# A two-layer graph kernel on one core: the instructions of its first two steps in another order, on four engines

## The reference

```python
h = relu(layernorm(x))
# layer 0, hypergraph convolution, twice; H = (adj != 0), w = first row of adj
Dn = 1 / (H @ w);  Be = 1 / H.sum(axis=0)
conv(h, W, b) = Dn * (H @ (Be * (H.T @ (h @ W.T)))) + b
y = conv(layernorm(relu(conv(h, W1, b1))) * gamma + beta, W2, b2)
x = x + y + h
# layer 1, attention by adjacency, three hops
X = relu(layernorm(x));  Xw = X @ Wv + bv
e = leaky_relu(sj + si + ab, 0.2)         # sj, si: Xw times two columns aw
T = adj * exp(e), rows normalized
x = x + relu(X @ Wk0 + T @ X @ Wk1 + T @ T @ X @ Wk2 + bk)
```

## Time and profile before

| | |
|---|---|
| median of 3 runs | 820.99 us (820.98 to 821.05) |
| the profiled execution's own time | 822.2 us |
| its span, first to last instruction | 820.4 us |
| busy in the span: TensorE products | 806.3 us (98%), 5782 instructions |
| VectorE | 641.8 us (78%) |
| ScalarE | 474.6 us (58%) |
| GpSimd | 425.5 us (52%) |
| mean granted clock of TensorE | 1.00 |
| HBM read, written | 49.03 MB, 8.39 MB |

### The profile page before, as it was taken

How to read it: one execution, slowest core, us unless ns; L and a number is a source line. 1 busy time by engine, 2 the same in 40 slices (tenths; PEclk the granted TensorE clock), 3 DMA queues, 4 the chain that set the end, 5 groups by cost and what they waited for, 6 DMA issues and landing times.

```text
span 820.4 us, 16724 instructions
## 1 busy us (share of the span) xinstructions
PE 806.3 (98%) x5782; PEld 752.5 (92%) x5782; DVE 641.8 (78%) x1738; ACT 474.6 (58%) x1005; POOL 425.5 (52%) x587
## 2 busy tenths in 40 slices
PE   7999999999999999999999999999999999999997
PEld 5878989999999999989999999999989999999997
DVE  6797788777789777887777789777887878777675
ACT  4348457483755737457483755737457483754745
POOL 2657482735737365482735737365482735732242
PEclk9999999999999999999999999999999999999999
DMA  8311204022130402204022130402205022110001
GB/s 294 129 66 53 90 1 167 2 91 77 36 130 0 157 9 77 89 0 166 0 86 80 34 132 0 153 13 77 89 0 166 0 80 87 35 70 1 26 5 49
DMA packets 39857, 57.84 MB, mean 71 GB/s; under 512 B 2576, under 2 KB 21008, under 8 KB 39824
## 3 DMA queue, kind: packets, MB, share of 16 engines
q1 hardware_dynamic: 39104, 57.42, 21.1%
q10 hardware_dynamic: 720, 0.01, 0.0%
HBM read 49.03 MB, written 8.39 MB: 70 GB/s over the span
## 4 chain that ended last, share of the span: by engine, by line
PE 91%; DVE 1%; ACT 0%; issue 0%; POOL 0%; DVEq 0%; POOLq 0%
PE ps L795 85%; PE ps L1014 3%; PE ps L943 2%; PE ps L990 1%; ACT xl L555 0%; DVE y L1212 0%; DVE x L1424 0%; DVE x L1217 0%; DVE part_a L1196 0%; DVE st_x L1430 0%; POOL rs_x L432 0%; DVE xt_lo L1223 0%; ACT r_sb L561 0%; DVE r_sb L1293 0%; ACT y_hi L588 0%
## 5 line engine op out<-in xcount | busy, mean ns | idle before, releaser
L406 POOL TENSOR_TENSOR y<-y,bk_row 128x256 f32<-128x256 f32 x64 | 56.6, 913 | 199.1 <-DVE a_lo L1323 190.2
L795 PE MATMUL ps<-w_hi,part_a 128*128 128x256 f32 (+1 forms) x512 | 156.5, 340 | 2.0 <-DVE part_b L1310 0.8
L795 PE MATMUL ps<-w_lo,part_a 128*128 128x256 f32 (+1 forms) x384 | 122.6, 319 | 0.0
L795 PEld LDWEIGHTS ps<-w_hi,part_a 128*128 128x128 f32 x512 | 96.2, 188 | 15.7 <-DVE part_a L1196 2.9
L795 PE MATMUL ps<-wk_hi,xt_hi 128*128 128x258 f32 (+1 forms) x256 | 89.1, 348 | 0.4 <-DVE xt_lo L1223 0.4
L795 PE MATMUL ps<-wk_hi,xt_lo 128*128 128x258 f32 (+1 forms) x256 | 86.7, 338 | 0.0
L795 PE MATMUL ps<-wk_lo,xt_hi 128*128 128x258 f32 (+1 forms) x256 | 86.6, 338 | 0.0
L795 PEld LDWEIGHTS ps<-w_lo,part_a 128*128 128x128 f32 x384 | 72.7, 189 | 5.6
L1317 DVE TENSOR_TENSOR e_sb<-e_sb,adjt_sb 128x512 f32<-128x512 f32 x64 | 44.3, 693 | 41.3 <-ACT e_sb L664 41.3
L470 POOL TENSOR_TENSOR xt_lo<-xl,xt_hi 128x256 fp32r<-128x256 f32 x60 | 56.7, 974 | 31.0 <-ACT xt_hi L738 31.0
L795 PE MATMUL ps<-w_hi,part_b 128*128 128x256 f32 x256 | 72.4, 283 | 0.0
(11 more groups left out here) (157 smaller groups left out, 2530.8 us busy)
## 6 DMA issues: line engine op xcount, KB each, us to landing
adj_sb<-in_adj SPq DMA_DIRECT2D x30, 512.0 KB, 5.9
adjt_sb<-in_adj_t SPq DMA_DIRECT2D x15, 1024.0 KB, 5.3
xin<-in_x SPq DMA_DIRECT2D x15, 512.0 KB, 4.6
out_dram<-x SPq DMA_DIRECT2D x15, 512.0 KB, 3.3
w_row<-in_adj SPq DMA_DIRECT2D x16, 256.0 KB, 3.4
adjt_sb<-in_adj_t SPq DMA_DIRECT2D x4, 256.0 KB, 7.0
e_sb<-in_w_t SPq DMA_DIRECT2D x2, 512.0 KB, 7.6
y<-in_wk SPq DMA_DIRECT2D x3, 256.0 KB, 7.4
```

Source lines behind the costliest of these rows:

```text
L406: pool.tensor_tensor(y10[:, t, D:], y10[:, t, D:], bk_row[:, :], ALU.add).then_inc(po_y0, 1)
L795: return pe.matmul(dst, stationary, moving, start=first, stop=last, skip_group_check=True)
```

## The change

It alters order and place in steps -1, 0 and 1 and leaves the loop's instructions alone, but for names.

- TensorE: both `keep_on` calls go. `products_of_weights` moves from behind z of step 0 to behind its y, into ps0, after all of lo_of_nt. The transposes of xl in step 1 move into z, ahead of its third tile, and go to ps1. The last group of the first m is issued tile by tile, and m of step 0 waits tile by tile.
- VectorE, step -1: be in two pairs, another place for the inct tiles. Step 0: the w2 low part goes; incidence tiles stand around the last z tile; lo_of_nt(1) comes after stats_r(3) and the means; h_lo_of stands ahead of g_tile; inct_of ahead of the row sums; x1 and its statistics ahead of row sums 2 and 3, with nb_x for batch 0 made here. Step 1: incidence, three stats_r and the means move behind si.
- GpSimd: makes the low part of w2; the skip sums of batch 0, the bk_row additions and the skip rows of batch 1 come later; wk_lo no longer waits for x1, and the root for x1 follows it.
- ScalarE: only c0_row is copied ahead of nt_hi, the other copies come after h_of; in step 1 xt_of precedes relu(1).

```diff
@@ -365,6 +365,12 @@
                    pattern=[[-1, P]], channel_multiplier=1).then_inc(su_pool, 1)
 pool.memset(f32(y2_hi[:, :, D:D2]), 1.0).then_inc(su_pool, 1)
 
+def skip_of_first(c):
+    pool.wait_ge(po_xb, c + 1)
+    pool.wait_ge(ac_hf, c + 1)
+    pool.tensor_tensor(skip[:, 0, c, :], skip[:, 0, c, :], h_f[:, c, :],
+                       ALU.add).then_inc(po_skip, 1)
+
 def rs_of_pair(s, lo_t):
...
 
+def rs_of_part(s, lo_t, made):
+    part = slice(lo_t, lo_t + TI)
+    wait(pool, dv_mvx, at(s, 1, made))
+    pool.tensor_scalar(v_x[:, part], mv_x[:, part, 1], EPS_LN, 1.0, ALU.add,
+                       ALU.mult).then_inc(po_vx, 2)
+    wait(pool, po_vx, at(s, 1, made))
+    pool.tensor_tensor(rs_x[:, part], v_x[:, part], minus_half[:, part],
+                       ALU.pow).then_inc(po_rsx, 2)
+
...
-    if s.next and s.k != -1:
+    def xb_of_next():
 
         wait(pool, ld_x, dma_at(s, 0))
         wait(pool, dv_x1, at(s, -1))
         for c in range(TI):
             pool.tensor_tensor(skip[:, o, c, :], xin[:, c, :], b2_row[:, :], ALU.add).then_inc(po_xb, 1)
+
+    if s.next and s.k not in (-1, 0):
+        xb_of_next()
     if s.k not in (-1, 0):
...
     if s.k == 0:
+        skip_of_first(2)
+        skip_of_first(3)
         rs_of_x(s)
         wait(pool, pe_m, at(s, 0))
         for t in range(TI):
             pool.wait_ge(ac_hf, TI + t + 1)
             h_hi_of(s, t)
+        pool.tensor_tensor(bk_row[:, :], bk_f[:, 0, :], bk_f[:, 1, :], ALU.add).then_inc(su_rows, 1)
+        pool.wait_ge(su_rows, 2)
+        pool.tensor_tensor(bk_row[:, :], bk_row[:, :], bk_f[:, 2, :], ALU.add).then_inc(su_rows, 1)
+        pool.wait_ge(su_rows, 3)
+        xb_of_next()
     if s.prev and s.here:
...
@@ -474,10 +492,10 @@
         for t in range(TI):
             skip_of(s, t)
         pool.wait_ge(su_wkhi, 1)
-        wait(pool, dv_x1, at(s, 0))
         for d in range(TD):
             pool.tensor_tensor(wk_lo[:, d, :], wk_f[:, d, :], f32(wk_hi[:, d, :]),
                                ALU.subtract).then_inc(su_wklo, 1)
+        rs_of_part(Step(4, 1, 1, NB), TI, 1)
     if s.prev and not s.here:
         y0_of(s, range(2))
     if s.prev:
@@ -501,19 +519,15 @@
     for c in range(TI):
         pool.wait_ge(ld_x0[c // 2], 16)
         pool.tensor_tensor(skip[:, 0, c, :], xin[:, c, :], b2_row[:, :], ALU.add).then_inc(po_xb, 1)
-    for c in range(TI):
-        pool.wait_ge(po_xb, c + 1)
-        pool.wait_ge(ac_hf, c + 1)
-        pool.tensor_tensor(skip[:, 0, c, :], skip[:, 0, c, :], h_f[:, c, :],
-                           ALU.add).then_inc(po_skip, 1)
     pool.wait_ge(ld_w, 16 * n_w)
     for c in range(TD):
         last = pool.tensor_scalar(bv_f[:, c, :], ones_f, bv_c[:, c:c + 1], 0.0, ALU.mult, ALU.add)
     last.then_inc(su_rows, 1)
-    pool.tensor_tensor(bk_row[:, :], bk_f[:, 0, :], bk_f[:, 1, :], ALU.add).then_inc(su_rows, 1)
-    pool.wait_ge(su_rows, 2)
-    pool.tensor_tensor(bk_row[:, :], bk_row[:, :], bk_f[:, 2, :], ALU.add).then_inc(su_rows, 1)
-    pool.wait_ge(su_rows, 3)
+    pool.wait_ge(su_w2hi, 1)
+    pool.tensor_tensor(w2_lo[:, :, :], w2_c[:, :, :], f32(w2_hi[:, :, :]),
+                       ALU.subtract).then_inc(su_w2lo, 1)
+    skip_of_first(0)
+    skip_of_first(1)
 
...
@@ -623,13 +637,8 @@
         relu(3)
         xt_of(1)
         if s.k == 0:
-            act.wait_ge(su_pe, 1)
-            act.activation(c_e[:, :], ps1[:, 2, 0:1], ACT.Identity, bias=ab_c[:, :]).then_inc(su_c, 1)
-            act.activation(c0_row[:, :], ps1[:, 0, 0:D], ACT.Copy).then_inc(su_c, 1)
-            act.activation(wk_f[:, :, D:D2], ps1[:, 1, 0:2 * TD].rearrange("p (a b) -> p a b", a=TD),
-                           ACT.Copy).then_inc(su_wk, 1)
-            act.wait_ge(su_c, 1)
-            act.activation(c_e[:, :], ps1[:, 2, 1:2], ACT.Identity, bias=c_e[:, :]).then_inc(su_c, 1)
+            act.wait_ge(su_bet, 1)
+            act.activation(c0_row[:, :], ps1[:, 0, 0:D], ACT.Copy).then_inc(su_c0, 1)
         if s.k != 0:
             h_of(3)
         relu_v(0)
@@ -755,11 +764,17 @@
     exp(3)
     y10_out(3)
     if s.k == 0:
+        act.wait_ge(su_w2lo, 1)
         for t in range(TI):
             y_hi(t)
-        act.wait_ge(su_w2lo, 1)
         for t in range(TI):
             h_of(t)
+        act.wait_ge(su_pe, 1)
+        act.activation(c_e[:, :], ps0[:, 2, 0:1], ACT.Identity, bias=ab_c[:, :]).then_inc(su_c, 1)
+        act.activation(wk_f[:, :, D:D2], ps0[:, 1, 0:2 * TD].rearrange("p (a b) -> p a b", a=TD),
+                       ACT.Copy).then_inc(su_wk, 1)
+        act.wait_ge(su_c, 1)
+        act.activation(c_e[:, :], ps0[:, 2, 1:2], ACT.Identity, bias=c_e[:, :]).then_inc(su_c, 1)
         g_hi_of()
         m_hi()
         act.wait_ge(su_wk, 1)
...
@@ -816,20 +832,14 @@
         last = mm(ps1[:, 3, 0:D], gam_f[:, c, :], w2_f[:, c, :], c == 0, c == TH - 1)
     last.then_inc(su_gam, 1)
 
-def keep_on(bank, times):
-
-    for _ in range(times):
-        mm(ps1[:, bank, 0:P], ident[:, :], ident[:, :], True, True)
-
 def products_of_weights():
 
-    keep_on(1, 8)
     pe.wait_ge(su_rows, 1)
     for d in range(TD):
         for c in range(TD):
-            mm(ps1[:, 1, 2 * d:2 * d + 2], wv_f[:, c, col(d)], aw_c[:, c, :], c == 0, c == TD - 1)
+            mm(ps0[:, 1, 2 * d:2 * d + 2], wv_f[:, c, col(d)], aw_c[:, c, :], c == 0, c == TD - 1)
     for c in range(TD):
...
+    def second_transposes():
+
+        for t in range(2):
+            wait(pe, ac_xl, at(s, -1, 2 * t + 1))
+            wait(pe, dv_x1, at(s, -1))
+            for j in range(2):
+                for d in range(TD):
+                    last = pe.transpose(ps1[:, t, col(2 * j + d)], xl[:, 2 * t + j, col(d)],
+                                        ident[:, :])
+            last.then_inc(pe_xt, 2)
+
     if s.prev2 and s.here:
         wait(pe, dv_x1, at(s, -1))
         v_tile(s, 0, ps1)
@@ -913,6 +934,8 @@
 
             if s.k == 0 and t == 2:
                 mean_of_gamma()
+            if s.k == 1 and t == 2:
+                second_transposes()
             for d in range(TD):
                 if t == 0:
                     wait(pe, dv_ulo, at(s, 0, 2 * d + 1))
...
@@ -952,11 +974,10 @@
     if s.prev:
 
         if s.k == 1:
-            keep_on(3, 8)
             pe.wait_ge(su_wklo, TD)
         for t in range(TI):
             bank = (t + 2) % 4
-            if s.here and t < 2:
+            if s.here and (t < 2 or s.k == 1):
                 wait(pe, dv_z, at(s, 0, bank))
             wait(pe, dv_xtlo, at(s, -1, t | 1))
             for d in range(TD):
@@ -1019,7 +1040,7 @@
 
         if s.k == 0:
             pe.wait_ge(su_w2lo, 1)
-            pe.wait_ge(su_c, 3)
+            pe.wait_ge(su_c0, 1)
         for t in range(TI):
             wait(pe, dv_ntlo, at(s, 0, t))
             if s.prev:
...
@@ -1034,21 +1055,28 @@
 
         for i in range(TI):
             pe.wait_ge(dv_inc, i + 1)
+            pe.wait_ge(h_hi_made, i + 1)
+            if i < TI - 1:
+                for t in range(TI):
+                    mm(ps0[:, t, 0:D2], inc[:, o, i, col(t)], h_hi[:, i, :], i == 0, False)
+            pe.wait_ge(h_lo_made, i + 1)
             for t in range(TI):
-                pe.wait_ge(h_hi_made, i + 1)
-                mm(ps0[:, t, 0:D2], inc[:, o, i, col(t)], h_hi[:, i, :], i == 0, False)
-            for t in range(TI):
-                pe.wait_ge(h_lo_made, i + 1)
+                if i == TI - 1:
+                    mm(ps0[:, t, 0:D2], inc[:, o, i, col(t)], h_hi[:, i, :], False, False)
                 last = mm(ps0[:, t, 0:D], inc[:, o, i, col(t)], h_lo[:, i, :], False, i == TI - 1)
                 if i == TI - 1:
                     last.then_inc(pe_m, 1)
 
     def m_stage():
 
-        wait(pe, dv_inc, at(s, 1))
-        wait(pe, h_lo_made, at(s, 1))
+        if s.k != 0:
+            wait(pe, dv_inc, at(s, 1))
+            wait(pe, h_lo_made, at(s, 1))
         for t in range(TI):
             for i in range(TI):
+                if s.k == 0 and t == 0:
+                    wait(pe, dv_inc, at(s, 1, i))
+                    wait(pe, h_lo_made, at(s, 1, i))
                 mm(ps0[:, t, 0:D2], inc[:, o, i, col(t)], h_hi[:, i, :], i == 0, False)
                 last = mm(ps0[:, t, 0:D], inc[:, o, i, col(t)], h_lo[:, i, :], False, i == TI - 1)
             last.then_inc(pe_m, 1)
@@ -1126,7 +1154,11 @@
     if s.k == -1:
         m_first()
     elif s.k == 0:
+        pe.wait_ge(dv_ntlo, TI)
+        products_of_weights()
         g_stage()
+        pe.wait_ge(su_c, 2)
+        pe.wait_ge(su_wk, 1)
         m_stage()
     elif s.next:
         m_stage()
...
+            pair = slice(2 * h, 2 * h + 2)
+            wait(dve, pe_m, at(s, 1, 2 * h + 1))
+            dve.tensor_scalar(be_cnt[:, pair], ps0[:, pair, D], 1.0, None, ALU.max).then_inc(dv_bec, 2)
+            dve.wait_ge(dv_bec, at(s, 1, 2 * h + 1))
+            dve.reciprocal(be[:, o, pair], be_cnt[:, pair]).then_inc(dv_be, 2)
```

(144 more changed lines are left out.)

3 lines of the change are left out of this document (1 added, 2 removed).

## The result

The kernel after takes **824.37 us** (median, 823.43 to 824.99 in 6 runs) against 821.07 for the kernel before in the same session: a ratio of 1.004, interval 1.0027 to 1.0053. The forecast was 816.1, in a range of 813.4 to 818.9. The kernel became slower by 3.3 us.

The account below looks back on a forecast made before the run. TensorE, 91% of the chain, was taken as the bound, with savings only in the first two steps' waits and filler. Terms summed to 4.9 us off 822.2, 817.3; the profiled execution stood 1.2 above the median, hence 816.1, range 813.4 to 818.9.

Parts of the forecast that it names:

- sign of being wrong: Whole kernel: the forecast would be wrong if idle time of TensorE appeared after 70 us.
- Opening, 0.75: First u and z: earlier start of u and low parts that keep up bring z 0.75 us earlier.
- Filler and products, 3.51 + 0.2: Between first z and y: filler and weight products leave, 3.51 us; ScalarE is freed of small copies, 0.2.
- Inside y, 0.1: First y: tile 1 is 0.75 us late, the old tile 3 wait and restart, 0.85, go; gain 0.1.
- the products, 0.4: Behind first y: weight products cost 1.36 us again but cover old waits before g and m; net gain 0.4.
- GpSimd between m and o, -2.25: First step: bk_row and skip additions ahead of g_lo on GpSimd make o 2.25 us late, between 1.0 and 3.1.
- Row sums, x1 and z, 2.75: Second step, u to y2: takes 11.45 us instead of 14.2, including a 1.0 wait in z; gain 2.75.
- y2 to the scores, -0.5 and -0.1: Second step: bank wait 0.3 and si 0.2 behind lose 0.5 us; VectorE's work moved behind si loses 0.1.
- Rival (4): Whole kernel: saving handed back later, or the change does not shift TensorE; 820.9 us, chance 0.04.
- Rival (3): TensorE's clock falls to 1.2 GHz at o's stops until z's, costing 6.9 us; 823.0, chance 0.03.
- Rival (2): First two steps: displaced work costs more (GpSimd 0.85, w2_lo 0.4, VectorE's late order 0.9); 818.2 us, chance 0.18.
- Rival (1): Before o: GpSimd is in time for g_lo, so 2.25 us comes back; 813.9, chance 0.2.

Follow-up runs that it names:

- 814.72: Kernel after with 32 idle memsets, incidence(1) behind lo_of_nt(0), root of x1 ahead of wk_lo, wk_lo held until the second u_lo, g_lo ahead of skip rows: 814.72 us.

## Why the prediction was wrong

The step that put the time on the other side of 821 is this one: "A microsecond taken out ahead of about 75 us stays out, because from there TensorE runs without a wait." The prediction put what the loop can lose at nothing, on the strength of its idle time before, 4.6 us. The runs showed that the loop lost 5.8: VectorE stood for 3.6 to 3.8 at each of five returns while instructions were loaded, because the change had moved its loop by four places. Before with four idle memsets, and nothing else, lost 4.5 in the same way. The prediction's own sign of being wrong, idle time of TensorE after 70, came true with 7.27.

The second failure lies ahead of si, where 2.3 was gained and not 5.0. TensorE's start of each stage in us; "padded" is after with 32 memsets (u starts 0.35 later with them), "814.72" the fastest version but one:

| stage | before | forecast | after | padded | 814.72 |
|---|---|---|---|---|---|
| u | 14.28 | 13.98 | 13.94 | 14.29 | 14.27 |
| behind z (filler before, then transposes nt) | 28.63 | 27.88 | 28.02 | 28.36 | 28.35 |
| y | 34.43 | 29.95 | 31.10 | 31.48 | 30.45 |
| y's end | 40.96 | 36.4 | 37.61 | 37.95 | 37.53 |
| m | 46.48 | 41.5 | 42.70 | 43.02 | 42.61 |
| u, step 1 | 54.10 | 51.4 | 54.40 | 53.17 | 50.35 |
| y2 | 68.31 | 62.8 | 65.70 | 65.58 | 61.84 |
| si | 72.78 | 67.8 | 70.45 | 70.33 | 66.80 |

**Opening, 0.75:** right but for 0.14; u took 4.07, not 3.89.

**Filler and products, 3.51 + 0.2:** the filler left, but y started 1.15 later than forecast. The step that failed here is "hidden, with 0.4 at the far end", for w2_lo on GpSimd, and with it "I cost it at nothing" for the incidence tile. Each was costed alone: w2_lo was ready at 28.9, as forecast, but it held up the tile on VectorE for 1.6, and lo_of_nt(0) with it. Moving the tile gave 1.03 back at y's start.

**Inside y, 0.1, and the products, 0.4:** right (y took 6.51 against 6.45 forecast, y's end to m 5.09 against 5.1).

**GpSimd between m and o, -2.25:** the mechanism was right, and so was the size: from m to the next u the padded form takes 10.15 and the version of 814.72, where g_lo does not wait for the skip rows, 7.74, so the stops cost 2.4. (By the prediction's own times, 48.25 less 46.1, the term should have been 2.15.) The skip rows were priced at 2.8 + 0.3, with 1.0 for inct, 4.1 in all, and took 4.24. Forecast from m to the next u was 9.9; padded it was 10.15, and in after 11.70, because 16 products ran 0.21 apart instead of 0.12 at the lower clock: 1.5.

**Row sums, x1 and z, 2.75:** the place and kind were right (a stop inside z, behind GpSimd's root), the size was not. Forecast was a stop of 1.0; it was 0.84 in after, where the slower o had already used up the time, and 1.94 in the padded form, where u started earlier. The root ended at 57.95 and not at 55.9. That is y's 1.15 handed down the queue, and what the skip sums and bk_row took beyond their plain time. It also hid most of the lower clock: after with one memset starts u at 14.02 and shows no fall, and its y2 starts at 65.28 against 65.70, so the 1.5 lost in o came out as 0.4.

**y2 to the scores, -0.5 and -0.1:** the first was -0.28. The second was -0.5: y of the second step waits 0.26 and restarts slowly.

The padded form, 818.53, lies inside the forecast range, but that is in part luck: by step 2 its trace is 2.0 ahead of before's where 4.9 was forecast, and the unexplained drift adds 0.85. **Rival (4)** had the gain handed back later, and the argument against it, "TensorE's idle from 74.67 on is 4.6 in 746, too little to swallow 4.9", was the faulty one: idle time that a kernel has does not bound what a change can add. I also took instructions that are not altered to cost what they did before. **Rival (3)** happened in its first half (the granted clock was 0.50 from 50.46 to 53.87, in one execution of six), at 0.4 in place of its 6.9; and the prediction's "by that rule stops of the length expected here are harmless" did not hold: the longest stop in the ten microseconds ahead of that fall was 0.95, and the measurement decides. **Rival (2)** named the right kinds of cost, and its 818.2 is within 0.4 of what the padded kernel takes, though not for its reasons alone. **Rival (1)** fell: o did wait for g_lo.
